# A filler matmul of the identity behind each sum of the last three message passes of a graph network

## What is computed

```python
edge_index = jnp.stack([src, dst])
h = jnp.maximum(_layernorm(x, axis=-1), 0.0)
x = x + _L0_gnn_ref(h, L0_gnn_weight, L0_gnn_bias, edge_index, edge_weight)   # hyperbolic messages
h = jnp.maximum(_layernorm(x, axis=-1), 0.0)
x = x + _L1_gnn_ref(h, edge_index, ...)                                       # softmax attention
h = jnp.maximum(_layernorm(x, axis=-1), 0.0)
x = x + _L2_gnn_ref(h, edge_index, L2_gnn_W, L2_gnn_a)                        # exp(-leaky_relu) attention
h = jnp.maximum(_layernorm(x, axis=-1), 0.0)
x = x + _L3_gnn_ref(h, src, dst, L3_gnn_w_neigh, L3_gnn_w_self, L3_gnn_b_self) # mean of neighbours
return x
```

## Time and profile before

| | us |
|---|---|
| median of three runs | 6288.4 |
| lowest and highest | 6282.08, 6293.55 |
| the profiled execution, its own time | 6344.26 |
| its span, first to last instruction | 6342.4 |

### The profile page before, as it was taken

One profiled execution on the slowest core, in us unless ns is written; L12 is line 12 of the kernel. 1 busy time (PEld: TensorE's weight loads), 2 busy tenths in 40 slices (PEclk: granted clock), 3 DMA queues, 4 the chain that ended last, 5 costly groups with the idle time before them and its releaser, 6 DMA issues. The chain is left out here.

```text
span 6342.4 us, 60836 instructions
## 1 busy us (share of the span) xinstructions
PE 3646.0 (57%) x11839; PEld 2363.0 (37%) x11839; DVE 3432.2 (54%) x10446; ACT 1895.3 (30%) x4579; POOL 3353.5 (53%) x3529
## 2 busy tenths in 40 slices
PE   3377777777117465555555565555565265655657
PEld 1255555555114233333333333333333133333335
DVE  4377777777643255555556544444445444444445
ACT  2244444444355233333324322222224200000001
POOL 0466666664000266666664366666663366666662
PEclk7688989999565566766767777777777577777768
DMA  2443444443101333333333444444444433333332
GB/s 65 116 110 107 112 109 111 110 109 82 41 0 35 91 93 91 93 93 90 93 90 100 141 115 114 112 113 113 113 115 122 136 99 97 98 92 95 100 91 82
DMA packets 302268, 616.99 MB, mean 97 GB/s; under 512 B 66538, under 2 KB 174951, under 8 KB 301928
## 3 DMA queue, kind: packets, MB, share of 16 engines
q0 software_dynamic: 168960, 467.01, 27.8%
q1 hardware_dynamic: 107624, 117.42, 6.0%
q10 hardware_dynamic: 25344, 28.85, 1.6%
HBM read 560.45 MB, written 52.57 MB: 97 GB/s over the span
## 5 line engine op out<-in xcount | busy, mean ns | idle before, releaser
L450 POOL DMA_INDIRECT X<-table,src_tab x2640 | 2504.0, 948 | 2199.2 <-DMA table<-H 872.6
L557 PE MATMUL psum<-X,onehot 128*128 128x259 f32 x5280 | 2048.7, 526 | 1392.4 <-DVE A L1069 1019.0
L1069 DVE SCALAR_TENSOR_TENSOR A<-A,same_tab,psum 128x259 f32 x3476 | 1675.1, 482 | 1986.1 <-remote 1036.8
L557 PEld LDWEIGHTS psum<-X,onehot 128*128 128x128 f32 x5280 | 1184.7, 251 | 2032.0 <-issue 1089.8
L440 POOL DMA_INDIRECT X<-table,src_tab x880 | 837.2, 951 | 585.6 <-issue 236.3
L694 ACT ACTIVATE onehot<-G,zero_col,ecols 128x128 f32<-128x128 bf16 x1760 | 738.3, 482 | 1095.4 <-remote 387.6
L566 PE MATMUL psum<-H,G 128*128 x1760 | 611.8, 435 | 262.3 <-ACT G L721 113.6
L546 PE MATMUL psum<-X,onehot 128*128 128x259 f32 x1760 | 609.1, 433 | 246.9 <-ACT onehot L694 154.1
L566 PEld LDWEIGHTS psum<-H,G 128*128 128x128 f32 x1760 | 358.6, 215 | 405.8 <-issue 349.2
L546 PEld LDWEIGHTS psum<-X,onehot 128*128 128x128 f32 x1760 | 360.7, 213 | 368.9 <-ACT onehot L694 189.9
L694 ACT ACTIVATE onehot<-onehot,zero_col,coef 128x128 f32<-128x128 bf16 x880 | 365.7, 481 | 326.5 <-DVE coef L1183 293.0
(11 more groups left out here) (326 smaller groups left out, 2766.8 us busy)
## 6 DMA issues: line engine op xcount, KB each, us to landing
X<-table,src_tab POOLq DMA_INDIRECT x3520
plain<-rows_dram SPq DMA_DIRECT2D x110, 256.0 KB
plain<-rows_dram ACTq DMA_DIRECT2D x176, 160.0 KB
table<-H SPq DMA_DIRECT2D x21, 906.5 KB, 7.0
x_dram<-X SPq DMA_DIRECT2D x21, 896.0 KB, 4.1
X<-x_dram SPq DMA_DIRECT2D x14, 896.0 KB, 11.1
X<-in_x SPq DMA_DIRECT2D x2, 6144.0 KB
table<-H SPq DMA_DIRECT2D x1, 6345.5 KB, 24.3
```

The costliest lines, as they stand in the source:

```text
L450: pool.indirect_dma_start(ring[:, s % SLOTS, :], None, table, bass.IndirectOffsetOnAxis(src_tab[:, s:s + 1], 0)).then_inc(sem(f"batch_in{s ...
L557: pe.matmul(psum[:, k % ACC_BANKS, 0:W], hots[:, k % HOTS, :], ring[:, k, :], start=True, stop=True).then_inc(sem("used"), 1)
L1069: stt(total, total, same, psum[:, t % ACC_BANKS, 0:W], ALU.mult, ALU.add).then_inc(sem("sum_added"), 1)
```

## The change

Behind each sum of the three passes TensorE gets one more matmul: the stationary operand is the bf16 identity, the moving one is the same identity four times over (512 columns), and the result goes into a whole bank that nothing reads: bank 5 in `softmax_sums` (q = 0), bank 7 in the other two. It waits for nothing and no semaphore is counted up by it. Because bank 5 must be unread in `softmax_sums`, the two small transposes of `turn_ends` now write 40 columns at the end of bank 7, and VectorE's two scans in `row_links` read them there.

```diff
             def sum_step(q, i, k):
...
                 pe.wait_ge(sem("sum_added"), i * SLOTS + ((q + 1) * S + k + 1))
                 pe.matmul(psum[:, k % ACC_BANKS, 0:W], hots[:, k % HOTS, :], ring[:, k, :],
                           start=True, stop=True).then_inc(sem("used"), 1)
+                pe.matmul(psum[:, 5 if q == 0 else 7, :], ident_b[:, :],
+                          ident_b[:, :].rearrange("p (o e) -> p o e", o=1).to_broadcast([P, 4, P]), start=True, stop=True)
...
             def turn_ends(n):
                 pe.wait_ge(sem("ends"), n)
                 pe.sem_inc(sem("pe_go"), 1)
-                pe.transpose(psum[0:1, 5, 0:GR], run_max[:, P - 1:P], ident[0:GR, 0:GR])
-                pe.transpose(psum[0:1, 5, GR:2 * GR], back_max[:, 0:1], ident[0:GR, 0:GR]).then_inc(sem("ends_t"), 1)
+                pe.transpose(psum[0:1, 7, 3 * P:3 * P + GR], run_max[:, P - 1:P], ident[0:GR, 0:GR])
+                pe.transpose(psum[0:1, 7, 3 * P + GR:3 * P + 2 * GR], back_max[:, 0:1], ident[0:GR, 0:GR]).then_inc(sem("ends_t"), 1)
```

More of the change, by code:

```diff
@@ L1397, in row_links @@
                 dve.tensor_tensor_scan(back_row[:, 0:GR][:, ::-1], no_back[:, bass.ds(s0, GR)],
-                                       psum[0:1, 5, GR:2 * GR][:, ::-1], -BIG, ALU.add, ALU.max)
-                chain(dve.tensor_tensor_scan(run_row[:, 1:GR + 1], no_pass[:, bass.ds(s0, GR)], psum[0:1, 5, 0:GR],
+                                       psum[0:1, 7, 3 * P + GR:3 * P + 2 * GR][:, ::-1], -BIG, ALU.add, ALU.max)
+                chain(dve.tensor_tensor_scan(run_row[:, 1:GR + 1], no_pass[:, bass.ds(s0, GR)], psum[0:1, 7, 3 * P:3 * P + GR],
                                              run_row[:, 0:1], ALU.add, ALU.max))
```

## The result

The changed kernel takes **6315.6 us** (median of 5 runs, 6309.6 to 6321.0), the kernel before beside it 6282.1. The ratio is 1.0049, 95% interval 1.0035 to 1.0063: **+0.5%, about +31 us** (+34 by the medians). The forecast was 6377, +89 us: the right side, almost three times too much.

What follows compares the result with a forecast made beforehand. The prediction took GpSimd's gather rhythm plus pauses for ring slots as the bound. Fillers in cold stretches added +89 us, all else 0: 6377 us against the median 6288.4, range 6100 to 6590, likeliest case 6310 to 6470.

Steps and rivals of the forecast that it cites:

- What bounds the kernel: Last three passes: gathers every 1.254 us on GpSimd, plus pauses for free ring slots costing 0.199 us per gather.
- the floor of 1104: Time in us of one pass of 880 gathers with no pause at all, against 1279 with pauses.
- The filler's price: TensorE: 0.42 us per filler at 1.2 GHz, 0.21 at 2.4 GHz; 554 to 1109 us of added work.
- No filler can run in a hold, so the clock still falls there.: TensorE: each filler stands behind its sum, the next sum waits for VectorE, so engines still come out at 1.2 GHz.
- hold: Stretch in which news of ended matmuls comes late: VectorE adds nothing, TensorE stops, GpSimd fills the ring; 6 to 9 us.
- stays below 0.8: Expected sign: the granted clock in the three passes remains under 0.8 with fillers.
- 2.2 fewer sums in each cold stretch, so pauses 1.17 times as often at the same length: 5.5 us stretches at 1.2 GHz with TensorE full: 4.3 sums instead of 6.5, costing +89 us.
- holds get shorter: Rival: TensorE's ends are let go sooner with more instructions or at 2.4 GHz; 5763 or 6026 us; chance 0.23.
- exposed everywhere: Rival: more instructions bring more holds, or one-hot and score chains wait behind fillers; +200 to +418 us; chance 0.17.
- No effect: Rival: VectorE sets the cold stretch and the fillers fit beside it; 6288, +-12 us; chance 0.14.
- The rival drawn from the Trainium skill: Part of the shorter-holds rival (0.23): activity releases the throttle, so cold-stretch sums cost 0.43 us, not 0.85.
- Two small transposes moved, ends of passes: Transposes moved from bank 5 to bank 7, and sums left after a pass's last gather: 0 each.

Runs made afterwards that it cites:

- s_near3: Changed kernel's filler in the softmax pass alone, only behind sums 8 to 19 of each twenty (528), among the small transposes: 6371.9 us, 1.0065 against the kernel before.
- s_away3: Changed kernel's filler in the softmax pass alone, only behind sums 0 to 7 of each twenty (352), away from the small transposes: 6348.8 us, 0.9999 against the kernel before.
- the series without pauses: Third and fourth series of runs, in which the kernel before took 5563.7 and 5563.8 us and the changed kernel, run in the fourth, 5564.6.
- f_last: Changed kernel with the filler in the third pass alone, small transposes still moved to bank 7: 6279.1 us, 0.9999 against the kernel before.
- g_thin: Kernel before, with every second batch of five gathers and the waits for them left out in the third pass: 5778.8 us, 0.9134.
- h_sum: Kernel before, with each fp32 sum of the three passes replaced by one bf16 matmul of constants: 6278.7 us, 0.992.
- a_again: The changed kernel itself, run again in the fourth series: 5564.6 us against 5563.8 for the kernel before, 1.0001.
- the second and the fourth series: Two of five groups of runs, each with the kernel before beside the others; it took 6340.5 us in the second and 5563.8 in the fourth.
- p_each: Kernel before, with GpSimd waiting for one free ring slot before each gather, not five before each fifth: 6324.1 us, 0.9973.
- the last series: Fifth series: fillers in the softmax pass alone, among the small transposes (6371.9 us) or away from them (6348.8), beside a kernel before of 6345.7.

## Why the prediction was right or wrong

**What bounds the kernel.** Right. The passes go at the gathers' rhythm plus the pauses. Where the pauses are absent, the passes fall to 1108 to 1130 us, close to the floor of 1104, and the kernel to 5564.

**The filler's price.** Right where it could be read. In the changed kernel the sum behind a filler starts 0.21 us after it when warm (5244.13 to 5244.34) and 0.43 us when cold (5265.02 to 5265.45), as taken. The formulas for the gap in the Trainium skill, "TensorE: Matmul & The Clock Gate", section "Back-to-back issue gap", which give 216 and 427 ns for 512 columns, agree with this trace.

**"No filler can run in a hold, so the clock still falls there."** Half right. TensorE still comes out at 1.2 GHz, but the holds are now broken up, and fillers do run between their gaps (5251.92 and 5258.22 us above). The claim of gaps of 6 us and more failed (from 21 to none in 5200 to 6200 us), and so did "stays below 0.8" in places (0.82 in 2300 to 3400 us).

**"2.2 fewer sums in each cold stretch, so pauses 1.17 times as often at the same length": the step that failed.** This is the term of the sum that was worth +89 us, and it measured +31 to +34. The number came true (214 to 250, 201 to 236), the length did not (2.24 to 2.04 us lost by each). And the number came true by luck. It went by array time, and the 128-column filler costs as much as the 512-column one (+29 us). It also took one cycle of 15 gathers for typical, while the counted 201 pauses in 2131 gathers are one for each 10.6; with that, 2.2 sums fewer would have made it 10.6 / 8.4 = 1.26 times as often. The rival "holds get shorter" ran at the same time and took back most of the added pauses' time: 1.17 times 480 us would be +82 us, and it was +30. I had set the two against each other as cases, and they were two parts of one.

**Bounds and rivals.** The half of "exposed everywhere" that named "the one-hot and score chains of the first pass" had the right place: two thirds of the cost lies in that pass, and `s_near3` against `s_away3` speaks for it. Its price of +200 to +418 came from the chain share of L557 and was far too high. "No effect" is what happens in the series without pauses.

**Clock.** The rival drawn from the Trainium skill, "TensorE: Matmul & The Clock Gate", section "What's actually happening", had the fillers hold the clock up. In this case's traces they did: 0.72 to 0.79 in the third pass, 0.87 with two, and 0.78 to 0.91 in the series without pauses. No kernel got faster by it. In the series without pauses the higher clock was worth nothing, with 793 gathers in 990 us at either; in the others it may have paid for part of the long filler's array time, since the short filler costs the same without it, and no run separates the two.

**Two small transposes moved, ends of passes**: 0, as `f_last` shows.

**Open.** What a hold is. It is absent after the last gather and in the thinned pass of `g_thin`, which still had 0.63 gathers a us; lighter sums on TensorE make the passes shorter (`h_sum`); and in two series the gaps stay short enough for the ring's 40 slots. In the series with pauses about half of GpSimd's waits end by an update that is missing from the records ("remote", 141 of 278 in the changed kernel; none in `a_again`). One candidate fits both, and no run here tests it: that writing the records of the instructions is itself slowed. The Trainium skill, "NOTIFIC — the notification-queue block", section "7.1 Overflow: three behaviours, one of which stalls the engine", says that this block holds its producers back rather than lose a record inside it. Nor is it the chip alone: the second and the fourth series carry the same chip number in the results, with 6340 and 5564 us for the same kernel.

## What to carry to other kernels

A filler that raises TensorE's clock is worth something only where TensorE's array time is on the path. Here another queue sets the rhythm (a gather each 1.25 us); without pauses a clock of 0.91 instead of 0.78 bought nothing, and with pauses each further instruction cost something. If fillers are wanted anyway, the last series speaks for keeping them away from the places where small dependent transposes pass between engines. The finer wait of `p_each`, one slot at a time, saved 17 us where there were pauses. And before a stall is explained from one trace, look whether it is there in another series, on this chip and on others.

## What I had not expected of the hardware

The same program took 5564, 6277 and 6340 us in different series, with little spread inside each. All of the difference is in the four passes with indirect gathers (the first 1156, 1351 and 1381 us; the fourth 1106, 1282 and 1294). A change that costs +31 us beside one costs +1 us beside another, where the pauses are missing.
